# Holding GpSimd's weight splits and zeroing until the rows are normalised, and turning rows between the context's keys

## What is computed

```
x = x + tanh(g_xattn[0]) * L0_xattn(layernorm(x), ctx)     # 32 heads of 128, 4 key/value heads
x = x + tanh(g_ffn[0])   * L0_ffn(layernorm(x))            # base weight + 8 low-rank experts, soft routing
x = x + tanh(g_xattn[1]) * L1_xattn(layernorm(x), ctx)     # 16 heads of 96, 4 key/value heads
x = x + tanh(g_ffn[1])   * L1_ffn(layernorm(x))            # 8 low-rank experts, top-1 routing
x = x + tanh(g_xattn[2]) * L2_xattn(layernorm(x), ctx)     # 32 heads of 16, 8 key/value heads
...                                                        # gated MLP, quantised product, quantised MLP
def _layernorm(x): return (x - mean(x)) / sqrt(var(x) + 1e-5)
```

## Time and profile before

| | us |
|---|---|
| median of 3 runs | 1407.55 |
| lowest, highest | 1407.03, 1411.15 |
| the profiled execution, its time | 1409.07 |
| its span | 1407.1 |
| its mean granted TensorE clock | 0.976 of full |

### The profile page before, as it was taken

How to read it: one execution, slowest core, us unless ns; L and a number is a source line. 1 busy time by engine, 2 the same in 40 slices (tenths; PEclk the granted TensorE clock), 3 DMA queues, 4 the chain that set the end, 5 groups by cost and what they waited for, 6 DMA issues and landing times.

```text
span 1407.1 us, 21133 instructions
## 1 busy us (share of the span) xinstructions
PE 1336.5 (95%) x8186; PEld 1087.6 (77%) x8191; DVE 926.2 (66%) x1352; ACT 603.7 (43%) x1046; POOL 501.9 (36%) x364
## 2 busy tenths in 40 slices
PE   6999999999999999998899999999899999799986
PEld 4989888988888889987798888889785444477733
DVE  5488778864588778874547784587665774434277
ACT  2444444443344444441244443444335778232252
POOL 5126345381126646425221544124433000333212
PEclk8999999999999999999999999999998999999989
DMA  5111111121011121020021122012104000462000
GB/s 187 45 49 49 59 35 52 51 64 46 15 55 50 45 72 42 16 94 20 14 76 46 29 64 68 12 39 61 31 1 131 1 1 2 124 155 87 1 0 30
DMA packets 55105, 70.94 MB, mean 50 GB/s; under 512 B 26672, under 2 KB 32976, under 8 KB 55008
## 3 DMA queue, kind: packets, MB, share of 16 engines
q1 hardware_dynamic: 55008, 69.60, 16.5%
HBM read 57.13 MB, written 5.37 MB: 44 GB/s over the span
## 4 chain that ended last, share of the span: by engine, by line
PE 84%; DVE 9%; ACT 3%; issue 2%; POOL 1%; DMA 1%; SPq 0%; DVEq 0%; ACTq 0%; POOLq 0%
PE ps L770 13%; PE ps L745 12%; PE ps L719 9%; PE ps L754 9%; PE ps L712 8%; PE ps L704 5%; PE ps L689 4%; PE ps L1697 4%; PE ps L1301 3%; PE ps L1327 3%; PE ps L1710 2%; PE ps L1283 1%; PE ps L1312 1%; PE ps L1402 1%; PE ps L1019 1%
## 5 line engine op out<-in xcount | busy, mean ns | idle before, releaser
L843 ACT ACTIVATE pT<-ps 128x768 fp32r<-128x768 f32 x192 | 156.0, 812 | 290.5 <-PE ps L754 289.2
L770 PE MATMUL ps<-pT,vv 128*128 128x256 f32 (+1 forms) x1728 | 251.3, 290 | 2.5 <-DVE oT L953 2.5
L946 DVE TENSOR_TENSOR pT<-ps,pT 128x768 fp32r<-128x768 f32 x192 | 183.8, 957 | 78.5 <-ACT pT L843 77.9
L745 PEld LDWEIGHTS ps<-kT,qT 128*128 128x128 f32 (+1 forms) x1152 | 201.2, 188 | 41.2 <-DVE qT L898 1.9
L745 PE MATMUL ps<-kT,qT 128*128 128x512 f32 (+3 forms) x1152 | 231.2, 336 | 1.5 <-DVE qT L898 1.5
L770 PEld LDWEIGHTS ps<-pT,vv 128*128 128x128 f32 (+1 forms) x1728 | 215.2, 180 | 3.1 <-DVE pT L946 2.9
L851 ACT ACTIVATE prob<-ps,rows_and_turned 128x768 f32<-128x768 f32 x192 | 172.2, 897 | 78.5 <-DVE rows_and_turned L934 78.5
L934 DVE TENSOR_REDUCE rows_and_turned<-ps 128x1 f32<-128x768 f32 x192 | 182.8, 952 | 24.3 <-PE ps L745 24.0
L630 POOL TENSOR_TENSOR wo<-raw,one 128x512 fp32r<-128x512 f32 (+1 forms) x48 | 49.9, 1040 | 412.0 <-PE ps L719 411.3
L719 PE MATMUL ps<-wo,oT 128*128 128x512 f32 (+1 forms) x576 | 169.3, 403 | 5.1 <-DVE x L888 2.4
L754 PE MATMUL ps<-ident,prob 128*128 128x128 f32 x1152 | 157.3, 272 | 2.9 <-DVE pT L946 2.9
(11 more groups left out here) (248 smaller groups left out, 1874.6 us busy)
## 6 DMA issues: line engine op xcount, KB each, us to landing
raw<-in_l_wq SPq DMA_DIRECT2D x44, 256.0 KB, 2.7
f2raw<-in_f_w SPq DMA_DIRECT2D x11, 776.0 KB, 4.8
rows_and_turned<-in_m_w SPq DMA_DIRECT2D x11, 768.0 KB, 4.3
raw<-in_l_wo SPq DMA_DIRECT2D x32, 256.0 KB, 2.7
raw<-in_l_wo SPq DMA_DIRECT2D x16, 192.0 KB, 2.5
w3gu<-rows_and_turned SPq DMA_DIRECT2D x11, 256.0 KB, 3.1
ctxraw<-in_ctxT SPq DMA_DIRECT2D x2, 1024.0 KB, 7.7
ctxn<-in_ctx SPq DMA_DIRECT2D x1, 2048.0 KB, 8.6
```

The source lines that it names most:

```text
L745: last = nc.tensor.matmul(sc[:, lo:hi], query(A, h, qp)[:, r * P:(r + 1) * P], keys(A, h // A.g)[0:hd, kp, b, lo:hi], start=(qp, kp) == PA ...
L770: last = nc.tensor.matmul(bank(6, 256, hd), vv[:, vp, b * VT + j, group % 2 * hd:(group % 2 + 1) * hd], pT[:, q % 2, pp, j, :], start=(j = ...
L843: nc.scalar.activation(turned_p(m, HI), ps[:, 4:6, 0:S // 2].rearrange("p a (j c) -> p a j c", j=3), ACT.Copy).then_inc(sem("att_pT_hi"), 1)
L946: nc.vector.tensor_tensor(turned_p(m, LO), ps[:, 4:6, 0:S // 2].rearrange("p a (j c) -> p a j c", j=3), turned_p(m, HI).bitcast(F32), ALU. ...
```

## The change

It has four edits.

1. In `att_pool`, behind the layer norm, GpSimd waits until that layer norm's rows are all normalised, in both attentions.
2. At the second attention's entry, TensorE turns rows 0 and 1, does the first half of the context's keys, turns rows 2 and 3, and does the second half.
3. The low split of `l2wq` is taken out of its place behind the second attention, and put behind the zeroing, where it waits for `f1_wh` (the routed `wh` of all four rows).
4. The zeroing waits for the four normalised rows (`rows_ready`), where it waited for the attention's last addition to `x` (`layer_done`).

```diff
@@ att_pool
                 if j == (0 if A is A0 else 2):
                     layer_norm()
+                    g.wait_ge(sem("rows_ready"), RT if A is A0 else 3 * RT)
 
             if A is A1:
                 att_wait(g, A, "scores", A.items)
                 att2_split_pool(g, l2wkv, l2wkv_raw, "l2_wkv", 1)
-                att2_split_pool(g, l2wq, l2wq_raw, "l2_wq", 2)
+                att2_split_hi_pool(g, l2wq, l2wq_raw, "l2_wq")
@@ att_pe
             else:
+                turn_row(pe, u, 0)
+                turn_row(pe, u, 1)
                 job(A.first[0])
+                turn_row(pe, u, 2)
+                turn_row(pe, u, 3)
                 job(A.first[1])
-                turn_pe(pe, u)
                 pe.wait_ge(sem("xT_lo"), 2 * RT)
                 job(A.first[2])
                 job(A.first[3])
@@ the split in two functions
-        def att2_split_pool(g, w, given, name, n):
+        def att2_split_hi_pool(g, w, given, name):
             g.wait_ge(sem(name), 16)
             nc.gpsimd.tensor_tensor(w[:, HI], given[:], one[:].unsqueeze(2).to_broadcast(given.shape),
                                     ALU.mult).then_inc(sem("l2_w_hi"), 1)
+
+        def att2_split_lo_pool(g, w, given, n):
             g.wait_ge(sem("l2_w_hi"), n)
             nc.gpsimd.tensor_tensor(w[:, LO], given[:], w[:, HI].bitcast(F32), ALU.subtract).then_inc(sem("l2_w_lo"), 1)
@@ att2_pool
-            g.wait_ge(sem("layer_done"), 3)
+            g.wait_ge(sem("rows_ready"), 4 * RT)
...
+            g.wait_ge(sem("f1_wh"), RT)
+            att2_split_lo_pool(g, l2wq, l2wq_raw, 2)
```

More of the change, by code:

```diff
@@ L1193, in att2_split_pool @@
                                     ALU.mult).then_inc(sem("l2_w_hi"), 1)
+        def att2_split_lo_pool(g, w, given, n):
             g.wait_ge(sem("l2_w_hi"), n)
             nc.gpsimd.tensor_tensor(w[:, LO], given[:], w[:, HI].bitcast(F32), ALU.subtract).then_inc(sem("l2_w_lo"), 1)
+        def att2_split_pool(g, w, given, name, n):
+            att2_split_hi_pool(g, w, given, name)
+            att2_split_lo_pool(g, w, given, n)
         def att2_sp(sp):
```

## The result

The changed kernel ran 1396.1 us in the median of 7 runs (1392.22 to 1401.59), the kernel before 1406.03 us beside it (7 runs, 1403.01 to 1411.15): a ratio of 0.9921, 95% interval 0.9896 to 0.9945. The change is faster, by 9.9 us between the medians; the ratio alone says 11.1 us (0.0079 of 1406), 7.7 to 14.6 by its interval. The forecast was 1400.0 us and 7.5 us of gain, range 1396.5 to 1404.3. The sign was right; the time came out 0.4 us under the range, at the place where rival 2 had put it (1396.1). Of the 3.9 us between the forecast time and the measured one, 1.5 are the kernel before itself, which ran 1407.55 us in the median that the forecast started from and 1406.03 here; the gain is off by 2.4. The profiled execution ran 1396.31 us, its span is 1394.3 us, so 12.8 us less than the span of the profile before.

A forecast was written before the change was run, and what follows sets the result against it. TensorE, busy for 95% of the span, was taken as the bound, so gains come from its waits at three entries. 3.0 + 3.5 + 1.0 = 7.5 us, from a 1407.55 us median to 1400.0 us; 8-in-10 range 1396.5 to 1404.3.

The forecast's parts named there:

- rival 2: Clock gives more: first attention's keys at full clock (2.45) and second MLP's late row (1.46); 11.4 us, 1396.1 us; chance 0.12.
- Part 1: First attention's entry: holding GpSimd's splits shortens the four normalisations, so the rows' keys start 3.0 us sooner.
- the high end: First attention's entry: the twelve key matmuls also lose their slow clock, 2.45 us more than the 3.0 taken.
- Rival 3: First attention's normalisations are slow by DMA traffic, not GpSimd; 4.5 us of gain left, 1403.05 us; chance 0.08.
- Part 2: Second attention's entry: turns between the context's key halves remove a 1.9 us wait; with clock, 3.5 us taken, bounds 1.9 to 3.55.
- its clock term: Second attention's entry: without the wait the rows' keys take 2.96 us instead of 4.61, counted as 1.65 us.
- Part 3: Second MLP's entry: moving the low split removes the wait for row 0's reciprocal; 1.0 us taken, bounds 0 to 2.5.
- The covers: Slack for delayed GpSimd work: 2.7 us for the first attention's value split, 0.7 us for the low split of `l2wq`.
- Rival 4: Slower: the first attention's held value weights come late, past 2.7 us of cover; 0.3% slower at 1411.8 us; chance 0.03.
- Rivals 1 and 2: The first: remaining waits cost slow matmuls, two jobs at 2.45 us leave 2.6, 1404.95 us; chance 0.15. The other: rival 2.
- the late row: Second MLP's entry: row 3's normalisation, stretched by the zeroing, counted at nothing; up to 1.46 us at full clock.

The follow-up runs named there:

- The filler kernel: Kernel before plus fourteen unread 128x512 matmuls in TensorE's waits at the first attention's entry, nothing held; 1403.76 us, ratio 0.9997.
- the first hold alone: Kernel before with one edit: GpSimd waits for the four normalised rows at the first attention's entry only; 1401.5 us, ratio 0.9981.
- the moves alone: Kernel before with only the low split of `l2wq` and the zeroing moved at the second MLP's entry; 1406.06 us, ratio 1.0004.
- the kernel with all fillers: Changed kernel plus unread matmuls in the third attention and at the entries of both MLPs and the first two attentions; 1396.11 us, ratio 0.9932.

## Why the prediction was wrong in size

**Part 1, mechanism right, size too small: the step that failed.** The forecast said 3.0 us, "I leave that loss as it is; the high end takes it away, 2.45 us more." The wait gave 3.36 us (the splits of `xT` began at 16.15, not 16.4, and the keys began at 18.69, not 19.05; that is 4.53 us behind the first normalisation, forecast 4.8). The clock gave 2.44 us (5.49 to 3.05), of which I had counted nothing. Together 5.8 instead of 3.0, and 6.3 by the medians of the kernels with and without the hold, which isn't sharp. The zero had no reason beside it. The prediction used the clock for the turns alone, which come "in the part of the stretch ahead of the fall of the clock", and took the place of the fall as given. But the fall hung on what TensorE did in the 5 us of long normalisations; with these gone, the clock no longer fell ahead of the keys in any of the six profiles with the hold (those with fillers left out), and in four of them it didn't fall in the keys either. The filler kernel shows it from the other side: long normalisations left in place, waits filled, keys at 3.06. The same profile of before had the hint: at the second entry I did count the clock behind a wait that goes (1.65 us), and at the first I didn't.

How much it gives is not the same in each execution. With the hold the keys took 3.05 or 3.06 us in four profiles and 4.60 or 4.61 in two; without it they took 5.24 to 5.49 in five (profiles with fillers at this place left out). With these counts the clock term is 0.9 to 2.4 us, and 3.4 + 1.9 (the mean over the six) would have been the better term.

The waits ahead of the first turn go with this. In the two profiles with the half slow keys TensorE had waited 1.19 and 1.42 us there, in the four others 0.36 to 0.80 us. The instructions up to the keys are the same in all six, but the context's keys ahead of the turns ended sooner in the two. So less waiting ahead of the keys and a later fall of the clock, or none, came together; six profiles don't prove that the one sets the other.

The Trainium skill's "TensorE: Matmul & The Clock Gate" (the HAM clock gate) says that the window of observation runs freely. By it the same instructions can meet the fall at different places. No run here shows that by itself, since the six profiles also differ in that wait, and the two profiles of the changed kernel are alike within 0.1 us.

**The mechanism behind the long normalisations stood.** Held back, GpSimd's splits leave them at 540 to 546 ns; let loose again, three of four are at 1262 ns and more. Rival 3 (DMA) fell: 542 ns at a DMA share of 0.47. The Trainium skill's "SBUF — State Buffer" (the rule on the shared port pair) states an exclusive lock: a VectorE operation in a two-port mode and a GpSimd operation keep each other out for a whole instruction. The trace agrees, 542 against 1262 ns; the mode of the normalisation stands in no row.

**Part 2: size right, its clock term half luck.** 3.5 forecast, 3.70 in the profile, 3.44 alone, 3.4 by leaving it out. The wait of 1.9 us goes in each profile with the turns. The 1.65 us of clock is what one profile of the kernel before had. In the six profiles without the turns the rows' keys were slow in two (4.60 and 4.61 us) and at 3.06 in four, while the first value job was slow in five (4.45 us). In the eight with the turns the keys were always at 2.96. What I hadn't seen: in the kernel before both jobs were slow, and the changed kernel has neither (2.96, 2.82). That is the further 1.62 us of the table. The edit of the turns alone leaves the value job at 4.45, and the first hold alone, which touches nothing there, brings it to 2.82:
```profile
698.16 2.82 PE L706 MATMUL ps<-wv,ctxT 128*128 128x192 f32 x24
```
That row is of the kernel with the first hold alone, whose keys were slow instead. All seven profiles with both the turns and the hold at this entry have the value job at 2.82. Whether the hold has a share in this stays open, since no run has the second hold by itself.

**Part 3: the wait as forecast, the total smaller than it can tell.** 1.0 forecast; the wait is 1.16 us shorter, VectorE no longer waits for row 0's reciprocal, and the shorter last normalisation bought nothing on TensorE, as counted. The other 1.03 us of this stretch in the changed kernel goes with the clock, since the moves alone didn't have it; at equal slow length they gave 0.66 us in all. By the totals the part is worth -0.2 to 0.9 us; what it gives at its place, the third attention's slow stretch can take back.

**The covers held.** The low split's cover was 0.71 us, forecast 0.7. The value split of the first attention ended 0.29 us ahead of the value job, where I had counted 2.7 us of cover. The split ended at 27.86, 0.4 sooner than counted (28.3), but TensorE was there at 28.15 and not at 31.0, mostly by the 2.4 us of clock that I had not counted. Rival 4 was 0.3 us from becoming a wait: a cover has to be counted at the high end of the gain, not at the likely one.

**Rivals 1 and 2.** Both are in the result. The clock gave 2.4 us at the first entry, 1.5 at the first MLP, 1.6 at the value job and 1.0 at the second MLP beyond what I counted, and took 2.3 us back in the third attention and behind. Rival 2 named only the first and priced the rest by the late row, which gave nothing; its 1396.1 us is half right in cause, and that its number is the measured one is luck: with 1406.03 for the kernel before, its 11.4 us would have given 1394.6. The shift moved jobs out of the slow stretches as well as into them; in the rivals I had priced only the way in.

**What stays open.** What sets off the third attention's slow stretch and what ends it. It was 13.7 us long in five profiles, 17.1, 20.5 and 30.7 in two each, 34.1 in one and 44.4 in two. About half of that length is lost, 7 to 22 us, and the spread of 15 us is nearly that between executions of the kernel before (17.3). Times and clocks go together there: beside the second timing of the changed kernel, the executions of the kernel before go from 1400.66 us at a mean clock of 0.983 to 1417.64 us at 0.967. That this stretch makes the difference is likely but not shown, since no kernel but the changed one has more than one profile. Filling TensorE there, in three kernels, didn't prevent it. So the gain is known no closer than by the two intervals, 7.7 to 14.6 and 6.9 to 14.5 us.

## What to carry to other kernels

A wait on TensorE costs its length and, where the clock falls with it, the slow half of the job behind it: look at the granted clock of that job before and at the same shape elsewhere, count both for every wait that goes, and keep the clock's part as a range, since the same instructions gave 3.05 and 4.61 us. Keep GpSimd's elementwise work away from VectorE's steps on the way to TensorE, and put independent matmuls between a turn and its use. When waits go, count the covers of everything else at the largest gain, and compare two profiles by landmarks, since a stretch that the edit doesn't touch can give or take as much as the edit.

## What the runs showed of the hardware

- The granted clock fell while TensorE had been busy for 6.70 of 6.70 us, in a stretch of matmuls without a recorded gap. In the kernel with all fillers it was 8.50 of 8.50 us, and the clock stayed at half for 44 us with TensorE always busy:
```profile
1060.00:1068.50 8.50, 8.50 (x27) 4.18 (x26) 5.99 (x10) 1.79 (x3) 7.60 (x2) 1.00 0.00 0
1068.50:1112.50 44.00, 44.00 (x209) 18.74 (x209) 21.96 (x36) 20.92 (x25) 3.51 (x1) 0.50 0.00 1
```
- Matmuls whose result nobody reads brought real ones to full speed at the entries (5.49 to 3.06 us for twelve), and still moved the time of the kernel by less than could be measured. In the profile with fillers at all entries two slow stretches further on were longer, 30.7 us each instead of 20.5 and 13.7; in the profile with fillers at the first entry alone none was.
- GpSimd's zeroing of 128x2048, which reads nothing, stretched a normalisation on VectorE to 2001 ns as a split did, and with the zeroing held back it took 547 ns at most.
